# One fused layer of cross attention, self attention and experts: rounding, bias tables and weight splits moved at both ends of the context loop

## The reference

```python
# x (1, 256, 512), ctx_1024 (1, 25088, 512)
def xattn(Q, K, V, Wq, bq, Wk, bk, Wv, bv):
    # proj: (x @ W.T + b).reshape(1, -1, 16, 64): two rows of 512 make one token of 16 heads of 64
    q, k, v = proj(Q, Wq, bq), proj(K, Wk, bk), proj(V, Wv, bv)
    scores = einsum('bhqd,bhkd->bhqk', q, k) / sqrt(64)
    return einsum('bhqk,bhkd->bhqd', softmax(scores), v)
def attn(x, w_in, offsets, amplitudes, sharpness): # 16 heads of 32
    k, v, q = split(einsum('bld,ed->ble', x, w_in))
    diff = offsets[:, :, None] - rel[None, None, :]        # rel = -(L-1) .. L-1
    t = sum(amplitudes[:, :, None] * exp(-abs(sharpness)[:, :, None] * diff * diff), axis=1)
    logits = q @ k.T / sqrt(32) + t[:, i - j + L - 1]
    return softmax(logits) @ v
x = x + xattn(layernorm(x), ctx_1024, ctx_1024, ...)
x = x + attn(layernorm(x), ...)
x = x + ffn(layernorm(x), Wg, W1, W2, W3)          # top 2 of 8 experts, hidden 1024
```

## Time and profile before

| what | us |
|---|---|
| median of 3 runs | 1514.27 (1514.09 to 1515.62) |
| profiled execution, its own time | 1518.69 |
| span of the profile | 1517.0 |
| TensorE busy (share of the span) | 1439.9 (95%) |
| VectorE, ScalarE, GpSimd busy | 1314.0, 1239.7, 958.1 |
| first unit of chunk 1 starts | 45.00 |
| last weighted sum of the context loop starts | 1263.95 |
| self attention's projection starts | 1272.18 |

### The profile page before, as it was taken

The page is one execution under the profiler, slowest core; times in us unless marked ns, Lnnn a source line. Parts: engine busy times, 40 slices in busy tenths (PEclk is TensorE's granted clock), DMA queues, the critical chain, the costliest instruction groups (busy, mean ns, idle before and its releaser), DMA issues.

```text
span 1517.0 us, 47836 instructions
## 1 busy us (share of the span) xinstructions
PE 1439.9 (95%) x17942; PEld 1226.9 (81%) x17942; DVE 1314.0 (87%) x1768; ACT 1239.7 (82%) x3039; POOL 958.1 (63%) x980
## 2 busy tenths in 40 slices
PE   6799999999999999999999999999999877599999
PEld 5688888888888888888888888888888765377776
DVE  7688888898988889888888989998898877888995
ACT  4688888888888888888888888888888765767883
POOL 6486778778787877778787877878786513500000
PEclk9899999999999999999999999999999997599999
DMA  4257565656656565656656565655657658866991
GB/s 187 57 113 141 111 145 119 143 125 131 136 113 138 116 145 117 144 127 126 138 111 141 117 143 121 141 128 121 138 111 140 110 125 228 180 228 240 341 328 45
DMA packets 460175, 220.40 MB, mean 145 GB/s; under 512 B 433856, under 2 KB 440000, under 8 KB 453328
## 3 DMA queue, kind: packets, MB, share of 16 engines
q1 hardware_dynamic: 459680, 218.22, 61.4%
q10 hardware_dynamic: 432, 1.32, 0.3%
HBM read 111.96 MB, written 0.56 MB: 74 GB/s over the span
## 4 chain that ended last, share of the span: by engine, by line
PE 82%; DVE 7%; ACT 3%; DMA 3%; issue 2%; SPq 2%; POOL 1%; ACTq 0%; DVEq 0%; POOLq 0%
PE ps_proj L1634 53%; PE ps_proj L1705 8%; PE ps_proj L1909 6%; PE ps_s L1685 4%; PE ps_o L1685 4%; PE ps_o L1925 3%; DMA pt_s<-p_s 2%; DVE wsp L1383 2%; PE ps_proj L1663 1%; ACT prob L822 1%; SPq L475 1%; DVE v_s L1193 1%; DVE cmax L1171 1%; DVE p_s L1184 1%; PE ps_proj L1925 1%
## 5 line engine op out<-in xcount | busy, mean ns | idle before, releaser
L1634 PE MATMUL ps_proj<-ctx_s,wk_s 128*128 128x256 f16 x4032 | 468.5, 274 | 17.6 <-POOL ctx_s L584 8.7
L1634 PE MATMUL ps_proj<-wv_s,ctx_s 128*128 128x256 f16 x4032 | 465.2, 273 | 2.7 <-DVE k_s L1199 2.7
L1634 PEld LDWEIGHTS ps_proj<-ctx_s,wk_s 128*128 128x128 f16 x4032 | 389.9, 98 | 76.3 <-issue 28.3
L1634 PEld LDWEIGHTS ps_proj<-wv_s,ctx_s 128*128 128x128 f16 x4032 | 387.8, 98 | 56.9 <-issue 9.7
L584 POOL TENSOR_TENSOR ctx_s<-t_f,ctx_s 128x512 f16<-128x512 f32 x192 | 220.2, 1157 | 270.3 <-ACT ctx_s L724 270.3
L822 ACT ACTIVATE prob<-ps_s,nmax 128x256 f32<-128x256 f32 x392 | 180.6, 473 | 117.1 <-DVE nmax L1178 117.1
L1184 DVE SCALAR_TENSOR_TENSOR p_s<-prob,p_s 128x1024 f16<-128x1024 f32 x196 | 256.8, 1310 | 22.5 <-ACT p_s L833 14.4
L833 ACT ACTIVATE p_s<-prob 128x1024 f16<-128x1024 f32 x196 | 214.4, 1094 | 1.1 <-DMA pt_s<-p_s 1.0
L584 POOL TENSOR_TENSOR ctx_s<-ctx_f,ctx_s 128x512 f16<-128x512 f32 x144 | 206.1, 1431 | 5.2 <-ACT ctx_s L716 5.1
L822 ACT ACTIVATE prob<-ps_o,nmax 128x256 f32<-128x256 f32 x388 | 180.7, 504 | 0.0
L1705 PE MATMUL ps_proj<-v_s,pt_s 128*128 128x64 f16 x4656 | 154.1, 194 | 11.3 <-DMA pt_s<-p_s 11.3
(11 more groups left out here) (247 smaller groups left out, 2391.3 us busy)
## 6 DMA issues: line engine op xcount, KB each, us to landing
ctx_f<-ctxt_dram SPq DMA_DIRECT2D x48, 1024.0 KB, 6.1
wst<-w_dram SPq DMA_DIRECT2D x96, 512.0 KB, 5.6
pt_s<-p_s SPq DMA_TRANSPOSE x408, 3.2
tisa<-tisa_scores SPq DMA_DIRECT2D x12, 256.0 KB, 5.5
w_in_f<-w_in_dram SPq DMA_DIRECT2D x2, 1024.0 KB, 7.4
w_f<-wk_dram SPq DMA_DIRECT2D x2, 512.0 KB, 6.4
ctx_f<-ctxt_dram SPq DMA_DIRECT2D x2, 512.0 KB, 7.8
w_f<-wv_dram SPq DMA_DIRECT2D x1, 1024.0 KB, 11.4
```

The lines of the kernel that those rows point to most:

```text
L1634: ins = pe.matmul(ps_proj[:, bank(h, role), sub * QUARTER:(sub + 1) * QUARTER], lhsT, rhs, start=(fresh and sub == 0 and t == 0 and i == 0 ...
```

## The change

Four parts. (1) In step -1 ScalarE does the second half of chunk 1's rounding ahead of chunk 0's V blocks. (2) The bias tables: VectorE makes only the columns (negated offsets, negated sharpness, scaled selectors), in step -1; GpSimd casts the positions in step 45; in step 47 ScalarE subtracts and GpSimd squares; in step 48 ScalarE takes the exponentials, with the sharpness as scale. (3) `w_in_f` has its own memory (the place it had is kept as `beneath_v`); its parts are loaded behind group 2 of steps 44 (K), 45 (V) and 46 (Q), without a wait. GpSimd scales K and Q in place (step 47) and makes their low parts (K in step 48, Q in step 49); ScalarE rounds K in the second half of step 47. V is split as before. (4) Scores of groups 0 and 1 of the last chunk stand between M7 and M3 of the last V; their maxima and group 0's exponentials move to step 47 too, scores 2 and 3 stand behind the first and second weighted sum of the last step, with banks to suit, and the sum of the tables and its store go behind scores 3 and the last transposes.

```diff
@@ def layer
         rel = sb("rel", [P, 2 * T], F32, cross)
         reli = sb("reli", [P, 2 * T], I32, cross)
+        w_in_f = {i: sb(f"w_in_f{i}", [P, DT, D], F32, cross) for i in (V, Q, K)}
         cross.close()
...
-        w_in_f = [sb(f"w_in_f{i}", [P, DT, D], F32, w_in) for i in range(3)]
+        sb("beneath_v", [P, 3 * DT * D], F32, w_in)
...
@@ SyncE, step(c, odd)
-                    for i, at, used in ((K, (NCH - 3, 0), LAST), (Q, (NCH - 2, 0), NCH)):
+                    for i, at in ((K, (NCH - 5, 2)), (V, (NCH - 4, 2)), (Q, (NCH - 3, 2))):
                         if isinstance(c, int) and (c, g) == at:
-                            sp.wait_ge(ctx_low, UNITS * used)
                             sp.dma_start(w_in_f[i][:, :, :], w_in_dram[i]).then_inc(w_in_loaded[i], 16)
-                    if isinstance(c, int) and (c, g) == (LAST, 1):
+                    if isinstance(c, int) and (c, g) == (LAST, 3):
                         sp.wait_ge(tisa_out, 1)
...
@@ GpSimd
+            def tisa_squares():
+
+                for g in range(2):
+                    pool.wait_ge(tisa_arg, g + 1)
+                    pool.tensor_tensor(out=tisa_e[:, g, :], in0=tisa_e[:, g, :], in1=tisa_e[:, g, :],
+                                       op=ALU.mult).then_inc(tisa_square, 1)
+
+            def w_in_scales(i):
+
+                pool.wait_ge(w_in_loaded[i], 16)
+                for half in range(2):
+                    rows = slice(2 * half, 2 * half + 2)
+                    pool.tensor_scalar(w_in_f[i][:, rows, :], w_in_f[i][:, rows, :], FW_SCALE, None,
+                                       ALU.mult).then_inc(w_in_scaled[i], 1)
+
+            def w_in_lows_p(i):
+
+                for half in range(2):
+                    rows = slice(2 * half, 2 * half + 2)
+                    pool.wait_ge(w_in_high[i], half + 1)
+                    pool.tensor_tensor(out=w_in_s[i][1][:, rows, :], in0=w_in_f[i][:, rows, :], in1=w_in_s[i][0][:, rows, :],
+                                       op=ALU.subtract).then_inc(w_in_low[i], 1)
...
+                    if isinstance(c, int) and c == LOOP_END + 1 and h == 0:
+                        pool.wait_ge(rel_ready, 1)
+                        pool.tensor_copy(rel[:, :], reli[:, :]).then_inc(rel_ready, 1)
+                    if isinstance(c, int) and c == NCH - 2:
+                        if h == 0:
+                            tisa_squares()
+                        w_in_scales((K, Q)[h])
+                    if isinstance(c, int) and (c, h) == (LAST, 0):
+                        w_in_lows_p(K)
+                    if isinstance(c, int) and (c, h) == (NCH, 0):
+                        w_in_lows_p(Q)
...
@@ ScalarE, step(c, odd)
                     if not after(c, 0):
+                        if h == 1:
+                            ctx_highs(1, 1, 1)
+                            sum_highs(1, 1, 1)
                         for g in range(NG):
                             plain_highs(h, g)
                         weight_sum_highs(h)
-                    if exists(c, 2):
+                    if exists(c, 2) and (h == 0 or after(c, 0)):
                         ctx_highs(c + 2, odd, h)
+                    if isinstance(c, int) and (c, h) == (NCH - 2, 0):
+                        tisa_args()
...
+                    if isinstance(c, int) and (c, h) == (NCH - 2, 1):
+                        act.wait_ge(unit_done, units_through(2 * LAST))
+                        for half in range(2):
+                            w_in_highs(K, half)
...
                         p_highs(c, 2 * h + 1)
+                    if isinstance(c, int) and (c, h) == (LAST, 0):
+                        tisa_exps()
+                    if isinstance(c, int) and (c, h) == (NCH - 2, 1):
+                        exps(LAST, 0, LAST % 2)
+                        p_highs(LAST, 0)
...
@@ VectorE, step(c, odd) and last_step
                         p_lows(c, 2 * h + 1)
+                    if isinstance(c, int) and (c, h) == (NCH - 2, 1):
+                        maxima(LAST, 0, LAST % 2)
+                        maxima(LAST, 1, LAST % 2)
...
-                    if isinstance(c, int) and c == LOOP_END + 1:
-                        tisa_args(h)
-                    if isinstance(c, int) and c == NCH - 2:
-                        w_in_lows(K, h)
...
@@ TensorE, step(c, odd) and last_step
                     weighted(0)
                     weighted(1)
-                    units(M7, M3, M4)
+                    units(M7)
+                    if isinstance(c, int) and (c, h) == (NCH - 2, 1):
+                        scores(LAST, 0, LAST % 2)
+                        scores(LAST, 1, LAST % 2)
+                    units(M3, M4)
...
-                scores(LAST, 0, odd)
-                scores(LAST, 1, odd)
+                weigh(LAST - 1, 2, 1 - odd)
                 scores(LAST, 2, odd)
-                tisa_scores()
-                weigh(LAST - 1, 2, 1 - odd)
                 weigh(LAST - 1, 3, 1 - odd)
                 scores(LAST, 3, odd)
+                tisa_scores()
```

76 lines of the change are left out of this document (38 added, 38 removed).

## The result

| comparison | before, median (runs) | changed, median (runs) | ratio |
|---|---|---|---|
| first | 1514.18 us (4) | 1503.28 us (4) | 0.9927 [0.991, 0.9944] |
| again | 1516.10 (11) | 1503.84 (6) | 0.9914 [0.9895, 0.9932] |
| a third time | 1515.57 (11) | 1503.28 (6) | 0.9923 [0.9911, 0.9936] |

The change makes the kernel faster by 10.9 to 12.3 us. I had forecast 21.0, and 1503.28 lies outside my range of 1488.5 to 1501.0. The direction was right and the size wrong.

A forecast was written before the change was run, and what follows sets the result against it. TensorE was taken to bound the loop's middle, so gains lay at its ends: 6.7 + 9.4 + 4.9 + 0.5 - 0.5 = 21.0 us off the 1514.27 median, forecasting 1493.3 us, range 1488.5 to 1501.0.

The forecast's parts named there:

- Start, forecast 6.7: Loop start: moving ScalarE's two roundings ahead of the V blocks gains 6.7 us, bounds 5 and 9.
- the whole chain moving by 7.2: Loop start: work through four engines comes 7.2 us sooner, chunk 1's fifth product at 55.2, TensorE still standing some 3.
- Bias tables, forecast 9.4: Two half steps from 1165.09: without VectorE's table operations, waits and half-clock products go, gaining 9.4 us, bounds 8 and 9.5.
- Loads, forecast 0 and 4.9: w_in loads cost 0 in their new steps; the half step from 1222.98 gains 4.9 us, bounds 3 and 4.9.
- The collision rival: Each of three w_in loads costs 4.9 us, 14.7 in all, giving 1508.0 us; chance 0.06.
- The end, forecast +0.5: Loop end: reordered last-chunk work and less shared transfers, net gain 0.5 us, bounds +5 and -2.3.
- two maxima out of the chain: Last chunk: VectorE does two maxima while it would have waited, gaining 2.8 us.
- last transposes don't share: Loop end: the last transposes no longer share with other transfers, gaining some 2.2 us.
- exponentials ahead of V's blocks: Loop end: group 0's exponentials and rounding on ScalarE stand before V's last three blocks, losing 3.0 us.
- GpSimd's K low parts: Loop end: two K low parts stand before chunk 48's first rescale, making GpSimd some 1.7 us late.
- the rival on GpSimd: Ten added two-operand GpSimd instructions stretch VectorE's splits at the end, costing 4.9 us: 1498.2 us; chance 0.20.
- Behind the projection, forecast -0.5: Rest of self attention: later bias loads and expert weights delay first transposes, losing 0.5 us, bounds 0 and 2.75.

The follow-up runs named there:

- the first part alone: Kernel before, with only ScalarE's context and sum roundings of chunk 1's second half moved ahead of chunk 0's V blocks: 1509.11 us, ratio 0.9958.

## Why the prediction was wrong

**Start, forecast 6.7: right in size, and that by luck.** The table gives 6.4, the first part alone 6.9 at M1. But the step that was to bring it, the whole chain moving by 7.2, came true only in part. I let ScalarE begin the exponentials at 51.7, since the maxima were there at 50.47 before. VectorE's two-operand work beside GpSimd's sums grew by 3.9 us and the column operations took 2.7 there, where I took 0.5 in all and under 1; so the first maxima started at 54.03 and the exponentials at 55.73. The fifth product started at 59.25 in the mean of three profiles against 63.3 in four with the old order, 4.1 us sooner and not 7.2. The other 2.3 came from its 36 products, which ran at the full clock in 4.09 and not in 5.91 to 6.59, behind a stall of 0.6 to 0.9 us and not 3, and that I had held to be out of reach.

**Bias tables, forecast 9.4: mis-sized, 7.7.** The waits on a low part went, as forecast. Of the 1.7 us missing, 0.7 are the base: I took one execution's 33.70, and four have 33.0 in the mean. The other 1.1 are the changed kernel's, which lies over the 24.2 that I gave it: in one of three profiles by the wait of 1.97 on a transpose, and by about 0.5 in the others. The clock's share varies most. I took 2.9 from the row of 6.98, and the same stall gave 5.54 in the next execution; a stall of 2.37 or 2.38 was followed by 36 products of 4.10 in two executions and of 5.77 in two others. The granted clock in these 36 products (third number from the end) was 1.00 and 0.57 in the first profile of before, that is 2.4 GHz and nearly 1.2, and 0.70 for both in the kernel with the first part alone (its second stall was 3.03 us), of which the first stands here:

```profile
1170.35:1174.45 4.10, 4.10 (x42) 3.70 (x43) 3.85 (x6) 4.08 (x12) 2.74 (x3) 1.00 0.52 106
1186.65:1193.63 6.98, 6.98 (x42) 5.03 (x43) 5.80 (x8) 6.93 (x23) 6.02 (x8) 0.57 0.10 20
```

```profile
1163.53:1169.30 5.77, 5.77 (x42) 4.49 (x43) 4.86 (x7) 5.75 (x17) 4.41 (x5) 0.70 0.33 68
```

**Loads, forecast 0 and 4.9: right in kind, 4.1.** The last half step without moved scores is 12.25 against 16.33 in the mean before. The collision rival is out at its price of 14.7. Whether a load costs a little stays open: a wait of 1.7 to 2.1 us on a transpose came in five of 14 executions, and the one run with K's load elsewhere doesn't settle it.

**The end, forecast +0.5: this is the step that failed.** Without loss the stretch would be 12.25 for the half step and 32.2 behind it, 44.45; it is 47.65, so the end costs 3.2. My sign for it, some 37 us from M1 to the end of the last weighted sum, came out at 40.9. Differences of neighbouring runs divide the loss:

| my item | forecast | measured | from |
|---|---|---|---|
| two maxima out of the chain | +2.8 | +1.0 | 45.60 - 44.57 |
| last transposes don't share | +2.2 | 0 | below |
| exponentials ahead of V's blocks | -3.0 | -3.1 | 47.65 - 44.57 |
| GpSimd's K low parts | -1.7 | -0.5 | 32.67 - 32.2 |
| bias exponentials and scores late | none | -0.7 | 45.60 - 44.92 |

(44.57 is the mean of the two runs with the exponentials back.) The items are steps from one run to the next, so that they add up to the 3.2, but for rounding, says nothing of their cause. Two of them belong together: the bias exponentials cost nothing in the changed kernel (47.65 with them early), only without the fourth part. With them early on both sides the moved maxima are worth 0.3 (44.76 - 44.47), so of +1.0 and -0.7 what counts is +0.3.

The loss on ScalarE was sized right. The gains against it, 5.0 in my sum, were not there. The last transpose did not get faster: TensorE's last weighted sum starts when it has landed, and it took 4.7 us from issue to landing, in the kernel before (issued at 1259.21) as in the changed one (1243.71); this row is the same in both:

```profile
pt_s<-p_s SPq DMA_TRANSPOSE x1, 4.7
```

Over all profiles it took 4.6 to 4.8, while the median of the nine transposes from 1240 to 1264 us before was 3.3. I had read the 3.2 us of the earlier trace rows as what the last one would need without other transfers. From the end of the last split to TensorE's start it is 6.5 us in the changed kernel, where it was 5.7: the last two splits now end 1.1 us apart, and SyncE issues the transposes behind them one by one, 1.35 us apart. And the maxima that VectorE does in idle time shorten a chain of which exponentials, splits and transposes are the rest. The wait that I missed, TensorE's 5.85 us for the addition, is the same 3 us seen from another engine: V's low parts, which ScalarE's exponentials delay, stand ahead of the addition. Taken away alone, it brought the last weighted sum 1.2 us sooner.

A slip in the rival on GpSimd, which changes none of this: of the ten added instructions that I counted there, the four scales read one operand, not two.

**Behind the projection, forecast -0.5: 0.3 gained**, within what executions differ.

**From the profile to the median: the second thing that failed.** I took the sum off the median as it stood. By the profiles the change gains 16; by the medians 10.9 to 12.3. The three profiled executions of the changed kernel (1501.79, 1501.09, 1500.67) are the fastest or second fastest of their sets, while most others lie near 1503 to 1505; the profiles of before lie at 1518.69 and 1515.73, above or at the middle of theirs. Where the changed kernel's slower executions spend their 3 to 4 us no profile of it shows. Waits on one transpose (0 to 2 us), the clock behind a stall (0 to 2.9) and the part behind the projection (243.1 to 245.8 over all kernels) are the places that vary between profiles. Two profiles of kernels that differ from it only near the end hint at them: the one with the bias exponentials early (1503.90 us) lost 3.4 in the two half steps, the one with the addition moved (1504.00) is 2.4 longer behind the projection. That the same happens in the changed kernel is not shown.

So of the 21.0 the end is 3.7 short, the bias tables 1.7, the last half step 0.8, the start 0.3; the middle and the part behind the projection are 1.6 better: 16.1. The other 4 to 5 lie between profile and median.

**The faster version.** The changed kernel with `exps(LAST, 0)` and its rounding back behind V's blocks has the lowest medians, 1498.70 and 1500.07 us, 17.6 and 15.5 below the kernel before beside it (two of the first five executions lay at 1503). By the ratio, 0.9897 and 0.9895, it can't be told from the kernel with the fourth part undone and the bias exponentials early (0.9896, 14.8 us). What is left of the fourth part is worth 0.3 to 1 us of stretch.

## What to carry to other kernels

When an order is changed near the end of a pipeline, follow the queue of each engine through the moved work up to the last instruction, and price gains by that chain; an idle engine that is given work sooner gains only if its result is what the chain waits for, as two maxima here were for a tenth to a third of what I gave. The length of a wait is not its price: 4.1 of the 5.85 us went away in one run, and 1.2 arrived at the end of the chain. Cut a stretch again at its last stations before you call such a gain nothing, since a change of clock behind it can hide it. And before a forecast rests on one profiled execution, line up a second one: the same stall cost 0 or 1.7 us afterwards.

## What I had not expected of the hardware

The clock behind a stall isn't a function of the stall's length alone: after 2.37 to 2.38 us idle the 36 products took 4.10, 4.10, 5.77 and 5.77 us, after 4.14 us 6.98 and 5.54, and after 1.97 and 2.07 us 4.09 and 5.76.

Beside GpSimd even VectorE's smallest operations are stretched, and in proportion the most: `nmax`, 128x4, takes 0.16 alone and 1.11 beside a low part of K; `last_base`'s addition takes 0.69, and 2.49 beside a low part of Q; the two `tsel` operations, which read one tensor, 0.36 and 1.38, so one input alone is no safeguard. GpSimd's own work varies too: two of its scales took 5.50, 6.85 and 7.55 us in three places. What they take alone no run shows.
